# Batch 0's last normalisation placed inside the last inverse transform of a convolution, attention and expert kernel

## What is computed

```
def _inorm(x, w=None, b=None):            # moments of one image over H and W
    mu, var = mean(x, (-2, -1)), var(x, (-2, -1))
    return (x - mu) * rsqrt(var + 1e-5) (* w + b)

# layer 0, on group-normalised x
p = spectral conv of the attended images
a  = _inorm(p + xa, attn_w, attn_b)
an = _inorm(a, norm2_w, norm2_b)
m = _fno_layer(an, m0cw, m0sw, inner_norm=True, act=True)     # "layer 1" of the kernel
m = _fno_layer(m, m1cw, m1sw, inner_norm=True, act=False)     # "layer 2" of the kernel
x = x + (_inorm(m, mon_w, mon_b) + a)

# layer 1, the tokens are the image rows: 4 batches, 4096 tokens of 128
t = tokens(x)
t = t + causal_attention(_ln_t(t), Wq, Wk, Wv)                # _ln_t: norm over the 128 of a token
t = t + experts(_ln_t(t), ...)                                # 64 experts, top 8 tokens of each
```

## Time and profile before

| | us |
|---|---|
| median of 3 runs (2038.74 to 2044.37) | 2044.34 |
| the profiled execution, its own time | 2038.2 |
| its span | 2036.4 |
| TensorE busy in the span | 1734.1 (85%) |
| VectorE busy | 1574.0 (77%) |
| ScalarE busy | 1038.2 (51%) |
| GpSimd busy | 435.0 (21%) |

### The profile page before, as it was taken

One profiled execution on the slowest core, in us unless ns is written; L12 is line 12 of the kernel. 1 busy time (PEld: TensorE's weight loads), 2 busy tenths in 40 slices (PEclk: granted clock), 3 DMA queues, 4 the chain that ended last, 5 costly groups with the idle time before them and its releaser, 6 DMA issues.

```text
span 2036.4 us, 30968 instructions
## 1 busy us (share of the span) xinstructions
PE 1734.1 (85%) x11550; PEld 1086.7 (53%) x11550; DVE 1574.0 (77%) x3154; ACT 1038.2 (51%) x1553; POOL 435.0 (21%) x457
## 2 busy tenths in 40 slices
PE   8773777998889985599999999999999999976767
PEld 8741222798789885244444544444444544434536
DVE  5786999538766688598879988799877888578435
ACT  4387000133545244377777666766667666772110
POOL 2243666100190071235810310013000000000000
PEclk9886999999899987699999999999999999988879
DMA  6550363000000050000100110001000000030586
GB/s 166 213 150 22 75 129 77 1 1 1 1 1 1 1 172 1 3 1 1 32 11 1 21 22 1 1 11 22 11 1 1 1 1 1 1 125 0 201 315 187
DMA packets 113682, 101.00 MB, mean 50 GB/s; under 512 B 39168, under 2 KB 91776, under 8 KB 112992
## 3 DMA queue, kind: packets, MB, share of 16 engines
q1 hardware_dynamic: 113536, 99.02, 17.2%
HBM read 80.27 MB, written 12.44 MB: 46 GB/s over the span
## 4 chain that ended last, share of the span: by engine, by line
PE 64%; DVE 16%; ACT 8%; issue 6%; DMA 3%; SPq 1%; POOL 1%; DVEq 0%; ACTq 0%
PE PS L473 5%; PE PS L475 5%; PE PS L474 5%; PE PS L492 5%; PE PS L494 5%; PE PS L493 5%; PE PS L1271 4%; PE PS L1344 4%; PE PS L1353 4%; PE PS L455 4%; DVE U L1046 4%; ACT V L1560 3%; PE PS L1496 3%; DMA V<-in_L_ffn_weight 3%; ACT Z L694 2%
## 5 line engine op out<-in xcount | busy, mean ns | idle before, releaser
L691 ACT ACTIVATE Z<-PS,MI 128x1024 f32<-128x1024 f32 (+2 forms) x288 | 300.3, 1043 | 256.0 <-PE PS L475 221.0
L877 DVE TENSOR_TENSOR DB<-Z 128x1024 f16<-128x1024 f32 (+2 forms) x288 | 332.1, 1153 | 96.8 <-ACT Z L694 52.8
L857 DVE TENSOR_REDUCE MI<-PS 128x1 f32<-128x512 f32 (+2 forms) x576 | 356.7, 639 | 39.2 <-PE PS L455 22.7
L694 ACT ACTIVATE Z<-PS,MI 128x1024 f16<-128x1024 f32 (+2 forms) x288 | 298.6, 1037 | 0.0
L1046 DVE TENSOR_TENSOR U<-A,PS 128x1408 f32<-128x1408 f32 x108 | 166.4, 1612 | 1.9 <-PE PS L1462 1.9
L652 POOL TENSOR_SCALAR Z<-U,Z 128x128 f32<-128x128 f32 x104 | 65.5, 643 | 360.5 <-PE PS L494 243.0
L1058 POOL TENSOR_TENSOR U<-A,U 128x1408 f32<-128x1408 f32 x36 | 113.9, 3193 | 89.1 <-DVE MI L1822 33.5
L1468 PE MATMUL PS<-U 128*32 128x352 f32 x1152 | 112.2, 486 | 0.1
L492 PE MATMUL PS<-Z,A 128*128 128x512 f16 (+3 forms) x288 | 104.5, 363 | 4.9 <-ACT CST L702 4.9
L492 PE MATMUL PS<-Z,V 128*128 128x512 f16 (+3 forms) x288 | 104.2, 362 | 4.0 <-ACT CST L702 4.0
L1353 PE MATMUL PS<-CST,DB 66*128 66x128 f32 x768 | 102.4, 278 | 5.7 <-DVE DB L1962 5.6
(11 more groups left out here) (423 smaller groups left out, 3677.1 us busy)
## 6 DMA issues: line engine op xcount, KB each, us to landing
V<-in_L_ffn_weight SPq DMA_DIRECT2D x32, 1024.0 KB, 7.7
A<-x_planes SPq DMA_DIRECT2D x24, 528.0 KB, 9.3
U<-in_x SPq DMA_DIRECT2D x16, 512.0 KB, 3.8
V<-in_x SPq DMA_DIRECT2D x4, 2048.0 KB, 13.9
Z<-in_x SPq DMA_DIRECT2D x16, 512.0 KB, 3.8
out<-U SPq DMA_DIRECT2D x16, 512.0 KB, 5.0
U<-e_planes SPq DMA_DIRECT2D x48, 132.0 KB, 7.2
x_planes<-Z SPq DMA_DIRECT2D x2, 1056.0 KB, 8.3
```

The source lines that it names most:

```text
L691: act.activation(EX32[u % 2][:, 0:w], s, ACT.Exp, scale=SCALE / (QUP * KUP), bias=pb).then_inc(sem("ex_ev"), 1)
L694: act.activation(EHI[u % 3][:, 0:w], s, ACT.Exp, scale=SCALE / (QUP * KUP), bias=pb).then_inc(sem("hi_ev"), 1)
L857: dve.tensor_reduce(bm[:, g % 2, t, k:k + 1], PS[:, 4 + chunk_no[c] % 2, 0:w], AX.X, ALU.max).then_inc(sem("ch_ev"), 1)
L877: dve.tensor_tensor(ELO[u % 3][:, 0:w], EX32[u % 2][:, 0:w], EHI[u % 3][:, 0:w], ALU.subtract).then_inc(sem("lo_ev"), 1)
```

## The change

The images are split for the last normalisation into batch 0 (T = 32 images) and batches 1 to 3 (96).

- Batch 0 inside the transform: VectorE makes its row moments at k = 11 (behind the statistics of group 8), TensorE the product of 64 columns at k = 16, where the token weights are made now too; VectorE takes weights and variance at k = 20, ScalarE the root at k = 22, VectorE scale and bias at k = 23. ScalarE normalises groups 0, 2, 4, 6 at its k = 25, 27, 29, 31, GpSimd groups 1, 3, 5, 7, and adds all eight to U. VectorE takes the token statistics of groups 0 to 6 at k = 27 to 33, that of group 7 behind the loop.
- Batches 1 to 3 in attention's prologue: row moments of 96 images at the second slot (-10), the product of 192 columns at the third (-9), variance at slot -7, root at slot -5, scale and bias at slot -3. Their normalisation stays where it was.
- VectorE normalises no group any more.

```diff
@@ -239,7 +239,8 @@
         MV = WS[:, 0:2, :].rearrange("p k n -> p (k n)")
-        root_args = [rc[:, 0:4], istat[:, 2:3], WS[:, 3, :], WS[:, 5, :], image_var, image_var, WS[:, 3, :]]
+        MVB = [WS[:, 0:2, 0:T], WS[:, 0:2, T:N]]
+        root_args = [rc[:, 0:4], istat[:, 2:3], WS[:, 3, :], WS[:, 5, :], image_var, image_var, WS[:, 3, 0:T]]
@@ -335,10 +336,7 @@
         def by_pool(g):
-            return g >= 8 and g % 2 == 1
-        def by_dve(g):
-            return g in (2, 5)
+            return g % 2 == 1
@@ -507,6 +505,9 @@
                     top_scores(c)
+                if s == slots.start + 2:
+                    pe.wait_ge(sem("mv_ready"), 3)
+                    pe.matmul(PS[:, 0, 0:192], ones, MVB[1], start=True, stop=True).then_inc(sem("mv_mm"), 1)
@@ -618,10 +619,8 @@
-            if by_dve(g):
-                pool.wait_ge(sem("mn_dve"), sum(by_dve(i) for i in range(g + 1)))
-            elif not by_pool(g):
-                pool.wait_ge(sem("mn_act"), sum(not by_dve(i) and not by_pool(i) for i in range(g + 1)))
+            if not by_pool(g):
+                pool.wait_ge(sem("mn_act"), g // 2 + 1)
@@ -630,6 +629,7 @@
                 if by_pool(g):
+                    pool.wait_ge(sem("fin_coef"), 1 if g < 8 else 2)
@@ -654,6 +654,8 @@
+            for g in range(8):
+                last_norm(g)
@@ -665,19 +667,26 @@
+            act.wait_ge(sem("fin_coef"), 1 if g < 8 else 2)
...
             def root_tokens(b):
-                act.wait_ge(sem("var_ready"), 8 + b)
+                act.wait_ge(sem("var_ready"), 9 + b if b else 8)
...
+            def root_images():
+                act.wait_ge(sem("var_ready"), 9)
+                act.activation(WS[:, 3, T:N], WS[:, 3, T:N], ACT.Sqrt).then_inc(sem("root_ready"), 1)
             def cast_high(c):
+                if c == 0:
+                    act.wait_ge(sem("i1_mm"), 3 * NIM)
@@ -722,6 +731,8 @@
                         cast_high(c)
+                if s == slots.start + 6:
+                    root_images()
@@ -794,7 +805,7 @@
-        def vector_l1(dve, st, image_stats, row_moments):
+        def vector_l1(dve, st, image_stats, row_moments, image_variance, image_coefs):
@@ -815,7 +826,7 @@
                 n = slice(NT * b, NT * b + NT)
-                token_norm(n, 8 + b)
+                token_norm(n, 9 + b if b else 8)
@@ -902,6 +913,13 @@
             for s in slots:
+                if s == slots.start + 1:
+                    row_moments(slice(T, N))
+                    dve.memset(lay[:, 0:1], 0.0).then_inc(sem("mv_ready"), 1)
+                if s == slots.start + 4:
+                    image_variance(slice(T, N), PS[:, 0, 0:192], 3)
+                if s == slots.start + 8:
+                    image_coefs(slice(T, N), 9)
@@ -931,7 +949,7 @@
             token_variance(slice(0, N))
-            token_norm(slice(0, N), 8 + B)
+            token_norm(slice(0, N), 9 + B)
@@ -1254,8 +1272,6 @@
             pool.wait_ge(sem("ax_ready"), 16)
-            for g in range(8):
-                add_images(pool, g)
@@ -1360,7 +1376,9 @@
                     columns(k)
-                    if layer == 2 and k == 12:
+                    if layer == 2 and k == 16:
+                        pe.wait_ge(sem("mv_ready"), 2)
+                        pe.matmul(PS[:, 1, 448:512], ones, MVB[0], start=True, stop=True).then_inc(sem("mv_mm"), 1)
@@ -1515,8 +1533,6 @@
                 inverse(layer)
-            pe.wait_ge(sem("mv_ready"), 2)
-            pe.matmul(PS[:, 0, 0:256], ones, MV, start=True, stop=True).then_inc(sem("mv_mm"), 1)
@@ -1608,6 +1624,11 @@
                             gelu(k - 2)
+                    if layer == 2:
+                        if k == 22:
+                            root()
+                        if k >= 25 and k % 2:
+                            last_norm(act, k - 25)
@@ -1630,12 +1651,6 @@
                 inverse_evacs(layer)
-            root()
-            act.wait_ge(sem("fin_coef"), 1)
-            for g in range(8):
-                if not by_dve(g):
-                    last_norm(act, g)
@@ -1912,6 +1927,23 @@
+            def image_variance(n, sums, done):
+                w = n.stop - n.start
+                dve.wait_ge(sem("mv_mm"), done)
+                later(dve.tensor_copy(WS[:, 2, n], sums[:, 0:w]))
+                later(dve.tensor_tensor(WS[:, 3, n], WS[:, 2, n], WS[:, 2, n], ALU.mult))
+                later(dve.tensor_tensor(WS[:, 3, n], sums[:, w:2 * w], WS[:, 3, n], ALU.subtract))
+                dve.tensor_scalar(WS[:, 3, n], WS[:, 3, n], EPS, None, ALU.add).then_inc(sem("var_ready"), 1)
+            def image_coefs(n, ready):
+                dve.wait_ge(sem("root_ready"), ready)
+                later(dve.reciprocal(WS[:, 3, n], WS[:, 3, n]))
+                later(dve.tensor_scalar(WS[:, 3, n], WS[:, 3, n], PAR["mon_w"], None, ALU.mult))
+                later(dve.tensor_tensor(WS[:, 7, n], WS[:, 2, n], WS[:, 3, n], ALU.mult))
+                dve.tensor_scalar(WS[:, 7, n], WS[:, 7, n], -1.0, PAR["mon_b"], ALU.mult, ALU.add).then_inc(sem("fin_coef"), 1)
@@ -1978,34 +2010,25 @@
                         fold_weights(dve, later)
-                    if layer == 2 and k == 18:
+                    if layer == 2 and k == 11:
+                        later(dve.memset(lay[:, 0:1], 0.0))
+                        row_moments(slice(0, T))
+                        dve.memset(lay[:, 0:1], 0.0).then_inc(sem("mv_ready"), 1)
+                    if layer == 2 and k == 20:
                         take_weights(dve, later)
+                        image_variance(slice(0, T), PS[:, 1, 448:512], 2)
+                    if layer == 2 and k == 23:
+                        image_coefs(slice(0, T), 7)
+                    if layer == 2 and k >= 27:
+                        dve.wait_ge(sem("x1_ready"), k - 26)
+                        image_stats(U, k - 27)
...
-            row_moments()
-            dve.memset(lay[:, 0:1], 0.0).then_inc(sem("mv_ready"), 1)
-            dve.wait_ge(sem("mv_mm"), 2)
-            later(dve.tensor_copy(mu, PS[:, 0, 0:128]))
-            later(dve.tensor_tensor(v, mu, mu, ALU.mult))
-            later(dve.tensor_tensor(e2, PS[:, 0, 128:256], v, ALU.subtract))
-            dve.tensor_scalar(v, e2, EPS, None, ALU.add).then_inc(sem("var_ready"), 1)
-            dve.wait_ge(sem("root_ready"), 7)
-            later(dve.reciprocal(v, v))
-            later(dve.tensor_scalar(v, v, PAR["mon_w"], None, ALU.mult))
-            later(dve.tensor_tensor(b2, mu, v, ALU.mult))
-            dve.tensor_scalar(b2, b2, -1.0, PAR["mon_b"], ALU.mult, ALU.add).then_inc(sem("fin_coef"), 1)
-            dve.wait_ge(sem("fin_coef"), 1)
-            for g in range(8):
-                if by_dve(g):
-                    for i in range(4 * g, 4 * g + 4):
-                        ins = dve.tensor_scalar(Vn[:, i, :], Vn[:, i, :], WS[:, 3, i:i + 1], WS[:, 7, i:i + 1], ALU.mult, ALU.add)
-                    ins.then_inc(sem("mn_dve"), 1)
-            for g in range(8):
+            for g in range(7, 8):
                 dve.wait_ge(sem("x1_ready"), g + 1)
-                ins = image_stats(U, g)
-            later(ins)
-            vector_l1(dve, st, image_stats, row_moments)
+                later(image_stats(U, g))
+            vector_l1(dve, st, image_stats, row_moments, image_variance, image_coefs)
```

## The result

The changed kernel takes 2044.8 us (median of 18 runs, 2042.3 to 2047.7); the kernel before takes 2041.3 (18 runs beside them, 2036.0 to 2046.2). The ratio is 1.002, 95% interval 1.0011 to 1.0028: 2.2 to 5.7 us slower, within the 0.3% that the prediction calls no change. The forecast was 2044.8 and +3.6 us.

A forecast was written before the change was run, and what follows sets the result against it. VectorE was taken to bound the kernel. The transform's -0.1 and the prologue's +3.7 gave +3.6 us on the profiled 2038.2, so 2041.8; half the distance between two places of runs made it 2044.8, range 2035 to 2052.

The forecast's parts named there:

- What bounds: Transform and attention: VectorE is nearly full, 0.17 us free per group in the transform, so work put there is queued.
- The moments at k = 11: Inside the transform: GpSimd's additions hold batch 0's eight operations until 764.1, so TensorE starts group 12 9.64 us late.
- What is held: VectorE beside GpSimd's additions: all eight moment operations are held; PSUM evacuations, L1970 and the statistics are not.
- The clock: Behind TensorE's stall at group 12: the granted clock falls to 0.50 for two groups, costing 3.06 us.
- Rival 2: Transform after the stall: two or more further groups pass at clock 0.50, +6.6 us or more; chance 0.22.
- Without stall and clock: End of the transform: without those two losses the token moments would start at 801.6 in place of 814.0.
- VectorE's sum: Group 18 to the token moments: VectorE's work adds up to 32.6 us, from 781.4 to 814.0.
- GpSimd's chain: End of the transform: GpSimd's adds and scalings end at about 810.5, ahead of VectorE, which wants group 7 at 813.
- The prologue: Attention's prologue: the three insertions for batches 1 to 3 together cost 3.7 us (2.2 to 4.9).
- Moments of 96 images and the product: Prologue, before the first query projection: operations slowed by GpSimd's scalings plus TensorE's product cost 1.3 us (0.3 to 2.3).
- Variance: Prologue: four operations right ahead of a VectorE operation on which TensorE waits cost 1.1 us in full.
- Coefficients: Prologue, ahead of L857: 1.7 us of work against 0.42 us of VectorE idle time costs 1.3 us.

The follow-up runs named there:

- experiment 2: Changed kernel with batch 0's moments at k = 18, behind GpSimd's additions of x, and their product and the token weights at group 18: 2029.4 us, ratio 0.9954.
- experiment 7: Changed kernel with weights and casts on ScalarE, batch 0's moments and later steps behind GpSimd's additions, prologue insertions moved earlier: 2020.6 us, ratio 0.9904 to the kernel before.
- experiment 4: Changed kernel with the prologue's variance, root and coefficients moved to earlier slots (-9, -9, -8), where VectorE waits anyway: 2041.0 us, ratio 1.0009 to the kernel before.
- experiment 1: Kernel before with only the eight moment operations of batch 0 added at k = 11, their result unused: 2053.2 us, ratio 1.0078.
- experiment 5: Kernel before with the four operations that fold the token weights on ScalarE at k = 7 in place of VectorE: 2037.2 us, ratio 0.9996.
- experiment 8: Changed kernel with each of GpSimd's 16 additions of x split into two halves: 2043.5 us, ratio 1.0007 to the kernel before.

## Why the prediction was right

It was right in sign, class and size, and most of its steps held. Times below are of the changed kernel's frame; its first column product is 1.73 us earlier than before's.

- **What bounds.** Right. From group 18 on VectorE has no idle time, and the transform's end is its queue.
- **The moments at k = 11.** Predicted end 764.1, that is 762.4 here; measured 762.2. The stall ahead of group 12: 9.64 predicted, 9.62 measured. The path to it was luckier than it looks: I had GpSimd pausing 0.39 us for its load, with a third and perhaps a fourth operation slipping through; in this profile there was no pause, the first took 1.01 us, and five were held. The sum is insensitive to that: eight steps of 2.3 us are more than was left of GpSimd's burst (its additions back to back), so the burst's end sets the price in either form.
- **What is held.** Right, also for the form of which I had no row: L1888, which reads one slice twice, took 2.29 us. The evacuation from PSUM, the four statistics and L2002 kept 1.11 (in before), 0.86 and 0.75 us among the additions.
- **The clock.** +3.06 predicted. Group 12 starts at 763.80 and group 14 at 769.90, 6.10 us for two groups in place of 3.63: +2.5. Rival 2, a low clock that lasts, didn't happen here.
- **Without stall and clock.** The prediction's 801.6 is not its 814.0 - 9.64 - 3.06 = 801.3; where the 0.3 comes from it doesn't say. As a stretch 801.6 is 76.6, and experiment 2 measured 76.85.
- **VectorE's sum.** 32.6 predicted from group 18 to the token moments; 811.64 - 779.22 = 32.4 measured. Group 18 was predicted at 781.4, 779.7 here, and taken at 779.2. The stretch was to shrink by 0.1 us and shrank by 0.8, mostly the clock's term.
- **GpSimd's chain.** Predicted to end at 810.5 (808.8 here), ahead of VectorE; it ended at 808.26, and VectorE asked for group 7 at 810.73. The predicted cover of 2.5 us was there. It goes when the coefficients come later: in experiment 7 GpSimd is last.
- **The prologue.** 3.7 predicted, 2.8 measured, with one term wrong. *Moments of 96 images and the product, 1.3:* measured 0.05 (to the first query projection 826.08 - 811.64 = 14.44 against 14.39 in before). The range 0.3 to 2.3 missed it. I had the eight operations held by GpSimd's scalings; none took more than 0.46 us, all eight 2.7, and the idle time there covered them and the product. *Variance, 1.1:* VectorE's operation on the second projection starts 20.05 us behind the token moments in place of 18.99, 1.06 more; right. *Coefficients, 1.3:* the lag is 845.51 - 811.64 = 33.87 in place of 31.75, so 1.06 more again, up to the first full top score's maximum (L868, in before L857); nearly right. *Not in the sum:* another 0.7 behind it. In before the clock was at 0.96 to 1.00 from 849 to 856; in the changed kernel it stayed at 0.50 until 856. That looks like rival 2's mechanism at another place, where work in pieces had already kept the clock low, but it is argued and not shown: in experiment 4 the clock was full from 845 to 851 and at 0.50 again from 852 to 856, and the second profile of the changed kernel had it full at 846 to 848 and at 0.50 from 850 to 858, with the same 48.8 us.
- **The level.** The prediction put the runs of before in two places and added half their distance, 3 us, to the profiled time. Eighteen runs show no two places but a spread of 10 us with the median at 2041.3. The half was a good guess for the wrong reason, and that the forecast met the median of 2044.8 to the tenth is luck: its own spread was -1 to +7 us.

The rows had shown the free place next to the ones chosen: VectorE waits 6.62 us ahead of the first projection, and 2.25 of the 2.8 us were to be had by using it.

The Trainium skill, "SBUF — State Buffer", section "Who interferes with whom", says that VectorE and GpSimd exclude each other on the ports that they share, and that whoever issues first keeps them for its whole instruction. The trace of the changed kernel agrees (2.23 to 2.30 us for each held operation, the length of one addition), and so do the operations of 0.2 to 0.3 us with the additions cut. Experiments 1, 5 and 8 go beyond it: an operation that asked first waited while up to twelve later instructions of GpSimd went ahead; what the runs measured decides there.

## What to carry to other kernels

Before small VectorE operations are moved under other work, look at what GpSimd does there: here one operation with its operands in SBUF cost 0.2 us alone and up to the rest of GpSimd's burst beside it, and behind it stands everything that VectorE feeds. Bound such a price from above by the burst's end, not by the number of operations, and put them behind it or on ScalarE; here a shift by seven groups turned +0.2% into -0.5%, and taking all held pieces away, with the prologue's insertions moved too, gave -1.0%. When an edit frees one engine, ask which operation now slides under the same burst.

## What the runs showed of the hardware

- A VectorE operation held by GpSimd can be passed over by many back-to-back instructions of GpSimd: 10.21, 15.30 and 5.86 us for operations of about 0.2. In other executions it gets in at each boundary (2.23 to 2.30 us with additions of 2.32). The program of experiment 1 showed both.
- GpSimd's instructions at half the length didn't bound the hold: 15.3 us beside instructions of 1.27 (one profile).
- The size of the held operation didn't matter: 32 columns took 2.23 to 2.30 us where 128 columns took 2.34.
- The loads of x went on at 268 GB/s with the additions cut, and the moments took 0.2 to 0.3 us each: it is GpSimd's operations that hold, not the transfers.
